# A recurrent learning step in a fused two-layer kernel: the tile sum goes from TensorE to GpSimd, and the gradient clip is written in fewer operations

## What is computed

```python
alpha = sigmoid(mean(xf @ alpha_w.T, axis=0))          # decay, one number per chunk
theta = sigmoid(xf @ theta_w.T) * BASE_LR              # rate, one per sequence and chunk
eta = sigmoid(mean(xf @ eta_w.T, axis=0))              # momentum, one per chunk
k = rmsnorm(silu(xc @ wk_w.T), k_norm_w);  v = silu(xc @ wv_w.T)

def step(carry, inp):                                  # scanned over the chunks
    mem, surp = carry                                  # mem = (w0, w1, ln)
    def loss_fn(p):
        return mean((v_c - (k_c + rmsnorm(silu(k_c @ w0.T) @ w1.T, ln))) ** 2 * th_c)
    grads = grad(loss_fn)(mem)
    total = sqrt(sum(sum(g * g) for g in grads))
    clip = minimum(1.0 / (total + 1e-06), 1.0)
    new_surp = eta_c * surp - grads * clip
    new_mem = (1 - alpha_c) * mem + new_surp
```

## Time and profile before

| | us |
|---|---|
| runs shown | 3575.06, 3583.59, 3578.9; median 3578.9 |
| profiled execution, its own time | 3552.92 |
| its span, first to last instruction | 3551.1 |

### The profile page before, as it was taken

How to read it: one execution, slowest core, us unless ns; L and a number is a source line. 1 busy time by engine, 2 the same in 40 slices (tenths; PEclk the granted TensorE clock), 3 DMA queues, 4 the chain that set the end, 5 groups by cost and what they waited for, 6 DMA issues and landing times. The chain is left out here.

```text
span 3551.1 us, 77379 instructions
## 1 busy us (share of the span) xinstructions
PE 3219.4 (91%) x30347; PEld 1869.3 (53%) x30347; DVE 2574.3 (72%) x5104; ACT 2074.0 (58%) x4205; POOL 829.8 (23%) x753
## 2 busy tenths in 40 slices
PE   6887699999998699999999999769999999999998
PEld 6776222222222377777777777535555444545454
DVE  5876788888888256776766776578787777777774
ACT  6774277777777444434434434227667776777676
POOL 3321101111010223423423423133333121112110
PEclk8998799999999899999999999879999999999999
DMA  4100211111110000110110110042322222111101
GB/s 141 28 13 3 58 55 46 55 55 37 55 43 28 27 25 23 33 35 22 33 35 22 33 35 22 22 89 59 67 59 42 57 55 57 38 51 46 49 27 29
DMA packets 180473, 151.89 MB, mean 43 GB/s; under 512 B 44388, under 2 KB 160900, under 8 KB 179972
## 3 DMA queue, kind: packets, MB, share of 16 engines
q1 hardware_dynamic: 172228, 140.43, 14.1%
q0 software_dynamic: 6144, 4.72, 1.0%
q10 hardware_dynamic: 1728, 1.57, 0.2%
HBM read 48.45 MB, written 32.65 MB: 23 GB/s over the span
## 5 line engine op out<-in xcount | busy, mean ns | idle before, releaser
L1406 DVE TENSOR_REDUCE b_maxima<-psum 128x2 f32<-128x1024 f32 (+3 forms) x768 | 773.1, 1044 | 216.0 <-PE psum L1238 205.7
L1344 ACT ACTIVATE b_prob<-psum 128x512 f32<-128x512 f32 (+2 forms) x1536 | 725.3, 526 | 316.6 <-PE psum L1271 303.5
L1406 DVE TENSOR_REDUCE c_maxima<-psum 128x2 f32<-128x1024 f32 x512 | 602.4, 1220 | 119.2 <-PE psum L1232 118.1
L1344 ACT ACTIVATE c_prob<-psum 128x512 f32<-128x512 f32 x1024 | 535.8, 602 | 186.3 <-PE psum L1264 186.3
L1871 PEld LDWEIGHTS psum<-consts_layer,a_hid 128*128 128x128 f32 x4096 | 476.2, 192 | 53.6 <-issue 53.3
L1871 PE MATMUL psum<-consts_layer,a_hid 128*128 128x128 f32 x4096 | 477.8, 274 | 0.0
L1861 PE MATMUL psum<-a_x1t,consts_layer 128*128 128x512 f32 x1024 | 461.3, 596 | 10.5 <-issue 10.2
L1928 ACT ACTIVATE a_hid<-psum,consts_layer 128x512 f32<-128x512 f32 x512 | 348.0, 687 | 206.5 <-PE psum L1861 199.6
L1264 PE MATMUL psum<-b_qa,b_ka 64*128 64x512 bf16 (+3 forms) x2048 | 359.3, 302 | 54.7 <-ACT b_prob L1344 52.4
L1286 PE MATMUL psum<-b_prob,b_v 128*32 128x512 f32 (+3 forms) x4096 | 385.5, 448 | 0.4 <-ACT b_prob L1344 0.2
L2073 DVE SCALAR_TENSOR_TENSOR a_acc<-psum,a_gprob,a_acc 128x128 f32<-128x128 f32 x512 | 143.8, 343 | 264.5 <-PE psum L1871 251.9
(11 more groups left out here) (343 smaller groups left out, 4241.4 us busy)
## 6 DMA issues: line engine op xcount, KB each, us to landing
b_qa<-b_part SPq DMA_DIRECT2D x192, 128.0 KB
c_qa<-c_part SPq DMA_DIRECT2D x96, 128.0 KB, 2.5
c_ka<-c_part SPq DMA_DIRECT2D x90, 128.0 KB, 2.5
b_ka<-b_part SPq DMA_DIRECT2D x90, 128.0 KB
consts_layer<-layer_in SPq DMA_DIRECT2D x1, 5419.0 KB, 18.4
m_xin<-x SPq DMA_DIRECT2D x16, 256.0 KB, 4.1
xnt<-m_xt SPq DMA_DIRECT2D x16, 256.0 KB, 2.7
c_xt<-xnt SPq DMA_DIRECT2D x16, 256.0 KB, 2.8
```

Of the source, the lines that this page charges most:

```text
L1344: self.nc.scalar.activation(out, src, ACT.Exp, scale=SCALE).then_inc(self.s.free, 1)
L1406: self.nc.vector.reduce_max(out, src, X).then_inc(self.m.free, 1)
```

## The change

The sum of the 8 tiles is made on GpSimd in three dependent adds: four tiles plus four, two plus two, one plus one, through a new tile `xpart`. TensorE's matmuls and ScalarE's copy are gone, and with them the semaphore `xs_copied` and hidden's wait for it. The rates `ths` are made negative by their constant, which turns the sign of all gradients, and the clip becomes 1 / max(total + 1e-6, 1), which has the same value with the other sign.

```diff
--- before.py
+++ after.py
@@ -212,6 +212,7 @@
         kt = sb("kt", [P, CT * P])
         prod = sb("prod", [P, GATES, D])
         xs = sb("xs", [P, D])
+        xpart = sb("xpart", [P, HT, D])
         stats = sb("stats", [P, CT, 6])
         mv = sb("mv", [P, CT, 2])
         var = sb("var", [P, CT])
@@ -270,7 +271,6 @@
         kt_ready = sig("kt_ready", per=2)
         kt_copied = sig("kt_copied", per=2)
         xs_ready = sig("xs_ready")
-        xs_copied = sig("xs_copied")
         prod_ready = sig("prod_ready", per=2)
         R_ready = sig("R_ready")
         logits_ready = sig("logits_ready")
@@ -329,9 +329,6 @@
         norm_ps = bank[7][:, INTER + D:INTER + D + 1]
         K_BANK = {1: (2, 3), 0: (4, 5)}
 
-        def xs_ps(n):
-            return bank[0 if n < 3 else 2][:, 0:D]
-
         def logits_ps(n):
             return bank[1 if n < 2 else 3]
 
@@ -407,15 +404,6 @@
                             last = nc.tensor.transpose(bank[4 + h][:, t * P:(t + 1) * P], kn[n % 2][:, h * HT + t, :], K("ident"))
                         last.then_inc(kt_ready.sem, 1)
 
-                def sum_x(n):
-                    if n in (1, 2):
-                        pe.wait_ge(xs_copied.sem, xs_copied.at(n, 0))
-                    elif n > 2:
-                        pe.wait_ge(dz_ready.sem, dz_ready.at(n - 3, 1))
-                    for t in range(CT):
-                        last = nc.tensor.matmul(xs_ps(n), K("ident"), xn[:, t, :], start=t == 0, stop=t == CT - 1)
-                    last.then_inc(xs_ready.sem, 1)
-
                 def logits(n):
                     pe.wait_ge(R_ready.sem, R_ready.at(n, 1))
                     if n == 1:
@@ -429,8 +417,6 @@
                     pe.wait_ge(kt_copied.sem, kt_copied.at(s, 2))
                     pe.wait_ge(mem0_ready.sem, mem0_ready.at(s, 0))
                     for h in range(2):
-                        if h == int(s > 0) and has(s + 2):
-                            pe.wait_ge(xs_copied.sem, xs_copied.at(s + 2, 1))
                         if h == int(s > 0) and has(s + 1):
                             pe.wait_ge(tg_ready.sem, tg_ready.at(s + 1, 1))
                         for t in range(HT):
@@ -511,17 +497,14 @@
                 pe.wait_ge(consts, 32)
                 transpose_x(0, 0)
                 transpose_x(0, 1)
-                sum_x(0)
                 project(0)
                 transpose_x(1, 0)
                 transpose_x(1, 1)
-                sum_x(1)
                 transpose_k(0)
                 project(1)
                 transpose_x(2, 0)
                 transpose_x(2, 1)
                 logits(0)
-                sum_x(2)
                 logits(1)
                 for s in range(NC):
                     hidden(s)
@@ -549,7 +532,6 @@
                     norm(s)
                     if has(s + 3):
                         transpose_x(s + 3, 1)
-                        sum_x(s + 3)
                     if has(s + 2):
                         logits(s + 2)
                 transpose_w1(NC)
@@ -610,12 +592,6 @@
                             act.wait_ge(z_ready.sem, z_ready.at(n, 0))
                         nc.scalar.activation(kt[:, h * HW:(h + 1) * HW], bank[4 + h], ACT.Copy).then_inc(kt_copied.sem, 1)
 
-                def copy_xs(n):
-                    act.wait_ge(xs_ready.sem, xs_ready.at(n, 1))
-                    if n > 0:
-                        act.wait_ge(prod_ready.sem, prod_ready.at(n, 0))
-                    nc.scalar.activation(xs[:, :], xs_ps(n), ACT.Copy).then_inc(xs_copied.sem, 1)
-
                 def gate_tanh(n):
                     act.wait_ge(logits_ready.sem, logits_ready.at(n, 1))
                     if n > 0:
@@ -681,14 +657,12 @@
                 normalise_x(0)
                 for h in range(2):
                     copy_xt(0, h)
-                copy_xs(0)
                 normalise_x(1)
                 project_tanh(0)
                 for h in (1, 0):
                     square_k(0, h)
                 for h in range(2):
                     copy_xt(1, h)
-                copy_xs(1)
                 scale_k(0)
                 copy_kt(0)
                 project_tanh(1)
@@ -698,7 +672,6 @@
                 for h in range(2):
                     copy_xt(2, h)
                 gate_tanh(0)
-                copy_xs(2)
                 gate_tanh(1)
                 scale_k(1)
                 for s in range(NC):
@@ -736,8 +709,6 @@
                             copy_xt(s + 3, h)
                     if has(s + 2):
                         scale_k(s + 2, (0,))
-                    if has(s + 3):
-                        copy_xs(s + 3)
                     if has(s + 2):
                         gate_tanh(s + 2)
                         scale_k(s + 2, (1,))
@@ -777,8 +748,16 @@
                         pool.wait_ge(R_ready.sem, R_ready.at(n, 0))
                     nc.gpsimd.tensor_tensor(prod[:, 0:CT, :], xn[:, :, :], over(K("gates", 0, D), CT), ALU.mult).then_inc(prod_ready.sem, 1)
 
+                def sum_x(n):
+                    pool.wait_ge(xn_ready.sem, xn_ready.at(n, 1))
+                    own.done(nc.gpsimd.tensor_tensor(xpart[:, :, :], xn[:, 0:HT, :], xn[:, HT:CT, :], ALU.add))
+                    own.done(nc.gpsimd.tensor_tensor(xpart[:, 0:2, :], xpart[:, 0:2, :], xpart[:, 2:4, :], ALU.add))
+                    if n > 0:
+                        pool.wait_ge(prod_ready.sem, prod_ready.at(n, 0))
+                    nc.gpsimd.tensor_tensor(xs[:, :], xpart[:, 0, :], xpart[:, 1, :], ALU.add).then_inc(xs_ready.sem, 1)
+
                 def mean_products(n):
-                    pool.wait_ge(xs_copied.sem, xs_copied.at(n, 1))
+                    pool.wait_ge(xs_ready.sem, xs_ready.at(n, 1))
                     nc.gpsimd.tensor_tensor(prod[:, CT:GATES, :], over(xs[:, :], 2), tiles(K("gates", D, 2 * D)), ALU.mult).then_inc(prod_ready.sem, 1)
 
                 def subtract_v(n):
@@ -791,13 +770,16 @@
                 deviations(0)
                 deviations(1)
                 pool.wait_ge(consts, 32)
+                sum_x(0)
                 theta_products(0)
                 mean_products(0)
                 key_deviations(0)
                 deviations(2)
                 subtract_v(0)
+                sum_x(1)
                 theta_products(1)
                 mean_products(1)
+                sum_x(2)
                 key_deviations(1)
                 for s in range(NC):
                     pool.wait_ge(mem_ready.sem, mem_ready.at(s, 0))
@@ -811,6 +793,8 @@
                     pool.wait_ge(dy_ready.sem, dy_ready.at(s, 2))
                     if has(s + 1):
                         subtract_v(s + 1)
+                    if has(s + 3):
+                        sum_x(s + 3)
                     if has(s + 2):
                         key_deviations(s + 2)
                     root(s)
@@ -851,7 +835,7 @@
                     nc.vector.tensor_reduce(R[:, :], prod[:, :, :], X, ALU.add).then_inc(R_ready.sem, 1)
 
                 def gates(n):
-                    k_th = 0.01 * 0.5 * 2.0 / (NB * CHUNK * D)
+                    k_th = -0.01 * 0.5 * 2.0 / (NB * CHUNK * D)
                     dve.wait_ge(tg_ready.sem, tg_ready.at(n, 1))
                     nc.vector.tensor_scalar(ths[n % 2][:, :], tg[:, 0:CT], 1.0, k_th, ALU.add, ALU.mult)
                     nc.vector.tensor_scalar(eb[n % 2][:, 0:1], tg[:, CT + 1:CT + 2], 0.5, 0.5, ALU.mult, ALU.add)
@@ -910,9 +894,8 @@
                     dve.wait_ge(norm_ready.sem, norm_ready.at(s, 1))
                     nc.vector.tensor_scalar(tot, norm_ps, 1e-36, None, ALU.max).then_inc(tot_ready.sem, 1)
                     dve.wait_ge(total_ready.sem, total_ready.at(s, 1))
-                    own.done(nc.vector.tensor_scalar(total, total, 1e-6, None, ALU.add))
+                    own.done(nc.vector.tensor_scalar(total, total, 1e-6, 1.0, ALU.add, ALU.max))
                     own.done(nc.vector.reciprocal(clip, total))
-                    own.done(nc.vector.tensor_scalar(clip, clip, 1.0, -1.0, ALU.min, ALU.mult))
                     dve.wait_ge(base_ready.sem, base_ready.at(s, 1))
                     nc.vector.scalar_tensor_tensor(w0t, g_w0, clip, base[:, 0:INTER], ALU.mult, ALU.add).then_inc(mem0_ready.sem, 1)
                     nc.vector.scalar_tensor_tensor(w1, g_w1, clip, base[:, INTER:2 * INTER], ALU.mult, ALU.add)
```

## The result

| | before | after |
|---|---|---|
| median of nine runs | 3578.9 us (3575.1 to 3583.6) | 3587.8 us (3586.2 to 3598.4) |
| ratio | | 1.0027, 95% interval 1.0017 to 1.0037 |
| span of the profiled execution | 3551.1 us | 3585.3 us |
| learning step ends (first instruction of the next stage) | 352.97 us | 358.42 us |

The account below looks back on a forecast made before the run. The prediction took each learning-step chunk to be bound by a chain of hand-overs, no engine being full. Loop -2.6, prologue +1.7 and TensorE's clock +1.6 gave +0.7 us, 3579.6 us against 3578.9, range 3571 to 3588.

Parts of the forecast that it names:

- prologue, start of hidden(0): Before the first hidden layer: GpSimd's queued adds and products delay ScalarE's normalisation and key scaling; +1.7 us, start near 52.4.
- chunk 0, with a slow hidden(0): First chunk: 0.40 us gained at its end, but its hidden layer slowed by TensorE's lower clock, +1.6 us.
- chunks 1 to 7: Rest of the loop: 0.40 us gained per chunk end with a tile sum, 0.19 us at each of the last three updates.
- The loop: All eight chunks: L438 starts 0.40 us earlier at five chunk ends, last three updates gain 0.19 us each; 2.6 us gained.
- TensorE's clock: At hidden(0): TensorE idles where it had 3.52 us of work, so that layer runs slower, +1.6 us; bounds 0 and +3.4.
- rival B: Chunk ends: a new TensorE hole of about 1.2 us lowers the clock, 1.3 us per chunk, five times; 3586.1 us, chance 0.07.
- I take it as not binding: Prologue: the third normalisation's wait for GpSimd's sum and products, given no cost as ScalarE's own queue ahead is longer.
- A: Rival: clock stays up in the prologue, projection L398 gains, GpSimd's adds don't delay the root; -3.6 us, 3575, chance 0.20.
- C: Rival: GpSimd's adds slowed 0.8 us per chunk beside VectorE, root 1.0 us late; 3583.6 us, chance 0.08 together with D.
- D: Rival: removing TensorE's tile sum brings nothing, something unseen covered it; +2.7 us, 3581.6 us, chance 0.08 together with C.

Follow-up runs that it names:

- after_again: The change measured again with nothing altered, beside the kernel before the change: ratio 1.0030, learning step ends at 363.08 us.
- after_third: The change measured a third time with nothing altered, beside the kernel before the change: ratio 1.0023, learning step ends at 360.81 us.
- sum_only: The change with the old rates and clip, so only the tile sum moves to GpSimd; ratio 1.0025 to the kernel before the change.
- filler_prologue: The change plus 8 unread matmuls at each former place of the tile sum on TensorE, in the prologue only; ratio 1.0006 to the kernel before.
- pe_prologue: The change with the first three tile sums back on TensorE and ScalarE, the loop's on GpSimd; ratio 0.9999 to the kernel before.
- late_consts: The change with the load of the layers' constants (6.4 MB) issued a turn later on SyncE's queue; ratio 1.0017 to the kernel before.
- before_again: The kernel before the change run against itself with no edit; ratio 1.0004, learning step ends at 353.58 us.
- clip_only: The kernel before with only the negative rates and shorter clip, tile sum left on TensorE; ratio 1.0003.
- filler: The change plus 8 unread matmuls at each of the eight former places of the tile sum on TensorE; ratio 1.0009 to the kernel before.
- filler_loop: The change plus 8 unread matmuls at the five chunk ends of the loop, none in the prologue; ratio 1.0003 to the kernel before.
- moved: The kernel before with the short clip and, from chunk 3 on, TensorE's tile sum made a turn later, in the mid-chunk hole; ratio 1.0004.
- short_filler: The change with the first three tile sums on TensorE and ScalarE, and 4 idle matmuls at five chunk ends; ratio 0.9991 to the kernel before.

## Why the prediction was wrong

The sum had three terms. Against the mean of the two traces of before (step ends at 353.28) and the three of the change (360.77), they came out so:

| term | forecast | measured |
|---|---|---|
| prologue, start of hidden(0) | +1.7 | +3.5 (54.60 - 51.12) |
| chunk 0, with a slow hidden(0) | -0.4 + 1.6 | +0.9 (38.70 - 37.81) |
| chunks 1 to 7 | -2.2 | +3.1 (267.5 - 264.4) |
| sum | +0.7 | +7.5 |

**The loop, right in its mechanism.** The place of the gain (L438 held by the queue), the wait that takes over, 0.15 us behind the weight, the adds' 2.6 us, the root 0.2 us late, and an undisturbed chunk 0.3 us shorter: all are in the trace nearly as the text said (0.4 us was forecast for the chunk).

**The step that failed is "TensorE's clock".** It charged the lower work of TensorE once, at hidden(0), and gave the loop nothing: rival B, a low stretch for the new hole, was put at 0.07 on the ground that a hole of 2.91 us stands in a chunk at full clock. But TensorE also waited 2.91 us at that place in the chunk of the earlier trace rows that ran at 0.91; the one row couldn't carry the argument:

```profile
183.19 1.11 PE L470 MATMUL psum<-consts_shared,m_dy 128*128 128x128 f32 x4 [2.91 <-DVE m_dy L898]
```

In seven traces with the loop's sum off TensorE and no filler in its place (after, after_again, after_third, sum_only, filler_prologue, pe_prologue, late_consts) chunks 1 to 7 take 265.7 to 268.8 us, mean 267.4; in the two with 8 filler matmuls, 262.3. The difference, 5.1 us, is of the size of the term's error of 5.3, but not all of it hangs on the chunk ends that were changed. Chunks 1 to 4 make 1.7 us of it (150.62 against 148.95) and chunk 5, which begins behind the last changed chunk end, 1.2 (37.7 against 36.5). The other 2.2 us are chunk 6 (38.3 against 36.1), whose hidden layer follows a chunk end without tile sum or filler in any of these kernels. That layer is slow in six of the seven, but also in before_again and clip_only, so this part may be chance. B's price of 1.3 us per low stretch was sound for the shorter ones; its condition, one in all five chunks, was not: one to two disturbed chunks of chunks 1 to 4 were enough to turn the gain into a loss, because one that catches the hidden layer too costs up to 3 us (chunk 2: 39.86 against 36.80). Of chunks 1 to 4 in those seven traces, 10 of 28 take over 38 us; in the five traces with the sum or the filler at the chunk end (before, before_again, clip_only, filler, filler_loop) it is 1 of 20. In chunk 2 of the change's first trace the clock was low in the middle as well, where L456 needs 1.11 us for 0.66:

```profile
151.02 1.11 PE L456 MATMUL psum<-consts_shared,m_dy 128*128 128x128 f32 x4 [2.92 <-DVE m_dy L882]
```

The Trainium skill, TensorE: Matmul & The Clock Gate, Part 1, says that full speed is what activity releases and not the default. The traces here agree, with 10 of 28 chunks against 1 of 20 as the number, and with hidden(0): it takes 5.28 to 6.38 us in all six traces that have neither the sum nor the filler on TensorE in the prologue, and 3.69 us in eight of the ten that have one of them. The two others, moved and short_filler, have 5.38 and 5.37, so that work doesn't ensure full speed. The forecast's +1.6 us for a slow hidden(0) was of the right size (1.6 to 2.1 us in the three traces of the change); the table's +0.9 for chunk 0 is less because a trace of before has a disturbed chunk 0 of its own, 38.48 us.

**The prologue term was half of what it should be.** Of the 3.5 us, the second normalisation and the scaling came as forecast (1.9 us at the scaling). The rest is two waits that I had set aside. "I take it as not binding" was wrong for the third normalisation in after_again, where ScalarE idled 0.63 us for GpSimd's products, and the stores behind the constants added 0.5 to 2.2 us of idle time ahead of the copies. In the prologue ScalarE's waits shift the loads too (the constants are issued at 26.79 us in place of 24.03), and the stores behind them come back as a wait.

**Rivals A and C** didn't come: the root was late, and the adds kept to 1.27, 0.73 and 0.46 us beside VectorE's L907 and L851 of before. A also read the projection's 5.40 us at 35.42 as half clock; the granted clock over that row is 0.68, so it ran at half only in part. **D** fell with the 1.30 us row.

**What stays open** is how the loss divides. The traces give the prologue 3.5 us and chunks 1 to 7 3.1, from two and three traces that differ by up to about 3 us among themselves. The ratios say that the loop alone (pe_prologue, 0.9999) costs nothing, and that filling the loop alone (filler_loop, 1.0003) takes nearly the whole loss away. Each ratio is uncertain by 3 us to either side. Shown is that the tile sum's move makes the loss, and that work for TensorE in its place, or a whole prologue, takes most of it back.

About 2 us of the 9.6 (0.27% of 3579) are not in the learning step of the traces; they are within the scatter of the other stages from trace to trace, and I leave them open.

## What to carry over

Work that TensorE does while it would otherwise wait isn't free to remove where some stretches already run at a lower clock: look at which ones do, and measure before you trust the saving. A filler that ends before the awaited operand arrives holds nobody; with it one of eight chunks (1 to 4 of two traces) was disturbed, against 10 of 28 with nothing in the place. In a prologue, an operation moved to another engine joins a queue whose later members, the DMA queue's too, all shift; follow each to its landing before calling it hidden.

## What was not expected of the hardware

With eight unused 128x128 matmuls at five chunk ends (1.95 us of TensorE each) chunks 1 to 7 took 262.3 us in both traces, against 265.7 to 268.8 without them. A stretch of low clock in the middle of a chunk may cost next to nothing (37.24 us at 0.95 against 37.13 at 1.00), while one that meets the hidden layer lengthens that from 3.69 to 5.38 us, all of it on the chain. Behind a standstill of 0.94 us with the tile sum ahead of it none of five hidden layers was slow; with standstills of 1.30 to 1.56 us behind lighter work 10 of 28 chunks were disturbed. A VectorE operation of 0.69 us took 1.22 beside one of GpSimd's. And the same program differs by 0.6% between chips, nearly all of it in one stretch of the second layer (459 to 463 us, or 484).
